# Row-halved score matmuls, a split ninth product, a longer lead and a new order of turns in a fused RWKV and attention kernel

## The chip, the cores and the metric

The kernel runs on one core of one Trainium2 chip. The metric is the device time of one execution in microseconds (us). Shorter is better. TensorE is called PE, VectorE DVE, ScalarE ACT, GpSimd POOL, and SyncE, which issues nearly all DMAs, SP.

## What is computed

Two branches are computed from one layer-normed input of 2 x 1024 tokens by 128 channels, and both are added to the input. The first branch is RWKV: a WKV recurrence over time, gates, and a channel mix. The second branch is attention with 16 heads of 8 channels and weights mixed from experts. Cut to what matters here:

```python
q, k, v = (shp(q), shp(k), shp(v))       # (2, 16, 1024, 8) each
attn = jax.nn.softmax(jnp.einsum('bhsd,bhtd->bhst', q, k), axis=-1)
ctx = jnp.einsum('bhst,bhtd->bhsd', attn, v)
x = x + rwkv(xn, ...) + svd_moe(ctx, ...)
```

## The kernel before, in words

Two heads make a pair, and there are 16 pairs. Every value of q and k is split into three bf16 parts (main, rest, rest of the rest). A float32 product of 8 channels is so made from 9 products of parts, in 72 rows of contraction. The parts are written to DRAM (`store_parts`, L421) and loaded back per pair, replicated, into `q_op` and `k_op` (`load_pair`, L382): 96 rows are used for the first scores and 99 for the second ones. There are four buffer sets for the pairs (`SETS`).

Scores are computed twice.

- **A scores** (`fill_place`, L1078, the matmul on L1091) have queries on the partitions. One bf16 matmul gives 128 queries x 512 keys in one of three PSUM banks (5, 6, 7). DVE reduces it to its maximum (`read_place`, L973, the reduction on L986). A pair has 32 of these and one more turn (k = 2), in which PE transposes the maxima of the pair before (L1084), and DVE copies them out (L982). POOL splits them into three bf16 parts (`split_max`, L557), and SP places them as rows 96 to 98 of `q_op` (`place_max`, L393), against rows of ones in `k_op`.
- **B scores** (`scores`, L1161, the matmul on L1166) have keys on the partitions and already hold the subtraction of the maximum. Two matmuls fill two banks, and ACT takes the exponential of both in one instruction (`exps`, L801). A second two banks make the double buffer.
- **Values** (`values`, L1170, the matmul on L1176): float32 matmuls of 32 columns, in four column groups of the array for 2 heads x 2 halves of the queries. They accumulate in bank 4, which ACT copies at the end of a pair (`copy_ctx`, L807). SP stores it (`store_ctx`, L407), and it is loaded again at the end (`load_contexts`, L459).

The main loop has 128 steps, 8 for each pair, in iterations of four pairs, which are 32 steps. The order is written out by hand. `one_step` (L1180) issues for PE in each step: A turn 0, B scores of head 0, A turn 1, B scores of head 1, A turn 2, the values of the step before, A turn 3 (in one step of eight also a fifth turn), then possibly a product.

```python
fill_turn(it, todo[0])
if step == 0:
    pe.wait_ge(max_in[j % 2], (it * 2 + j // 2 + 1) * 16 * PARTS)
scores(p, j, step, 0)
fill_turn(it, todo[1])
scores(p, j, step, 1)
fill_turn(it, todo[2])
```

Products (`product`, L1138) are the float32 matmuls of the RWKV branch. An iteration has seven steps with one product (mean, var, cr and ck0 to ck3, at steps 17, 18, 22, 23, 25, 26 and 27) and one step (29) with cv, which is four in a row. They take a turn in the same rotation of three banks. The RWKV branch also gives DVE two scans after the A turns of each of the steps 2, 6 and 12 (L945), and work to ACT and POOL in many steps (`branch`).

Each A turn waits until DVE, or whoever takes a product, has read the turn three places earlier (`wait_for_bank`, L344). PE takes its instructions in order, so everything behind such a wait stands too. The A scores run ahead of the B scores by one pair and `LEAD` = 12 turns. This lead of 45 turns is computed before the loop, beside the projections of the RWKV branch (L1112, L1100).

SP has one queue in program order. Before the loop it stores the parts of batch 0, loads pairs 0 to 2 (12 DMAs), stores the parts of batch 1 (8 DMAs), stages v of pair 0 (`stage_v`, L400) and places the maxima of pair 0. In the loop it has 13 DMAs for each pair.

Of the kernel before, what the change touches and what calls it, by code (L numbers as in the profile page):

```python
# [6 lines left out]
P = 128  # L7
TILES = B * T // P
CHUNK = 512
# [6 lines left out]
ROWS = PARTS * PARTS * HD  # L16
MAX_ROW = 96
# [3 lines left out]
LEAD = 12  # L21
SPLIT_STEP = 5
# [24 lines left out]
def build(nc, x, cols, mats, rows, gw1, gb1, gw2, gb2, out):  # L47
# [4 lines left out]
    with ctx:  # L52
# [55 lines left out]
        q_op = sb("q_op", [P, SETS, 2, T], BF16)  # L108
        k_op = sb("k_op", [P, SETS, 2, T], BF16)
# [14 lines left out]
        ctx_dram = nc.dram_tensor("ctx_dram", [PAIRS, 4, HD + 1, CHUNK], F32).ap()  # L124
# [131 lines left out]
        op_in = [[sem(f"op_in{s}{e}") for e in range(2)] for s in range(SETS)]  # L256
# [67 lines left out]
        for t in range(SETS * KEY_TILES):  # L324
            at = A_PLACES + LEAD
            here = places(at + A_PLACES * t // KEY_TILES, at + A_PLACES * (t + 1) // KEY_TILES)
            place_turns.append(range(len(turns), len(turns) + len(here)))
            turns += here
            turns += [name for name, step in PRODUCT_STEP.items() if step == t]
        assert (len(turns) + 1) % 3 == 0  # L330
# [50 lines left out]
        def _(sp):  # L381
            def load_pair(p, s):  # L382


                for e in range(2):
                    sp.dma_start(q_op[0:ROWS, s, e, :],
                                 bass.AP(q_dram.tensor, (p * 2 + e) * (PARTS * HD * T),
                                         [[0, PARTS], [T, PARTS * HD], [1, T]])).then_inc(op_in[s][e], 16)
                    sp.dma_start(k_op[0:ROWS, s, e, :],
                                 bass.AP(k_dram.tensor, (p * 2 + e) * (SLOTS * HD * T),  # L390
                                         [[HD * T, PARTS], [T, PARTS * HD], [1, T]])).then_inc(op_in[s][e], 16)

            def place_max(p, s):  # L393

                sp.wait_ge(max_parts_ready, p + 1)
                for i in range(PARTS):
                    sp.dma_start(q_op[MAX_ROW + i:MAX_ROW + i + 1, s, :, :],
                                 max_parts[:, s % 2, i, :]).then_inc(max_in[s % 2], 16)

            def stage_v(p, s):  # L400

                for e in range(2):
                    sp.dma_start(v_op[:, s % 2, :, e, 0:HD],
                                 V[:, bass.ds(p, 1), :, HD * e:HD * e + HD].rearrange("p o k d -> p (o k) d")
                                 ).then_inc(v_in[s % 2], 16)

            def store_ctx(p, s):  # L407
                sp.wait_ge(ctx_copied, p + 2)
                for g in range(4):
                    sp.dma_start(bass.AP(ctx_dram.tensor, (p * 4 + g) * ((HD + 1) * CHUNK),  # L410
                                         [[CHUNK, HD + 1], [1, CHUNK]]),
                                 ctx_sb[32 * g:32 * g + HD + 1, s % 2, :]).then_inc(ctx_out[s % 2], 16)
# [8 lines left out]
            def store_parts(b, t):  # L421

                for slot in range(SLOTS if t else PARTS):
                    sp.dma_start((k_dram if t else q_dram)[b * HEADS:(b + 1) * HEADS, slot, :, :],
                                 parts[:, t, slot % PARTS, 2 * b:2 * b + 2, :].rearrange("p n t -> p (n t)")
# [24 lines left out]
            def rest(p, j, it):  # L450
                if not isinstance(p, int) or p + 3 < PAIRS:
                    sp.wait_ge(b_ready, p * 16 + 1)
                    load_pair(p + 3, (j + 3) % SETS)
                if not isinstance(p, int) or p + 1 < PAIRS:
                    sp.wait_ge(pv_done, p * 8 + 1)
                    stage_v(p + 1, (j + 1) % SETS)
                    place_max(p + 1, (j + 1) % SETS)

            def load_contexts(b):  # L459

                for s in range(2):
                    sp.wait_ge(ctx_out[s], 64 * (PAIRS // 4) * (b + 1) + 1)
                for hs in range(2):
                    at = (b * (HEADS // 2) * 4 + hs) * (HD + 1) * CHUNK
                    head_step = 2 * (HD + 1) * CHUNK
# [23 lines left out]
        def _(pool):  # L489
# [21 lines left out]
            g.memset(q_op[:, :, :, :], 0.0).then_inc(cleared, 1)  # L511
# [759 lines left out]
```

## Time and profile before

| what | us |
|---|---|
| median of 3 runs (527.71 to 529.12) | 528.16 |
| span of the profiled execution, first to last instruction | 526.2 |
| median less span | 1.96 |
| PE busy, of the span | 470.9 (89%) |
| DVE busy | 407.4 (77%) |
| ACT busy | 356.4 (68%) |
| POOL busy | 183.4 (35%) |

The profiled execution has no other time on record than its span. Busy time counts the time in which at least one instruction of an engine was under way. Matmuls overlap one another, so their mean duration is longer than the time from the start of one to the start of the next. A line of the timeline merges instructions of one kind that follow each other, with their count behind an x.

### The profile page before, as it was taken

What the parts mean: (1) busy time and instruction counts of PE and PEld (TensorE: products, weight loads), DVE (VectorE), ACT (ScalarE), POOL (GpSimd) and SP (SyncE); (2) the same over time, 40 slices, a digit from 0 to 9 for tenths busy, and PEclk for the clock granted to TensorE, in tenths of its full rate; (3) what the DMA queues carried; (4) which work ended last, traced back from release to release, by engine and by line L of the source; (5) the groups of instructions that cost most, each with busy time, mean ns of one, the idle gap of its engine ahead of it and who ended that gap; (6) DMA issues with size and microseconds to landing.
All of it is one profiled execution on the core that took longest, in us unless ns stands there. A gap on an engine that the chain in (4) does not pass through costs nothing.

```text
span 526.2 us, 8110 instructions
## 1 busy us (share of the span) xinstructions
PE 470.9 (89%) x2358; PEld 160.8 (31%) x2358; DVE 407.4 (77%) x668; ACT 356.4 (68%) x452; POOL 183.4 (35%) x214
## 2 busy tenths in 40 slices
PE   5339379999999999999999999999999999999992
PEld 3115123232233332222333322223333223232252
DVE  3578989999888868998887689998876899981022
ACT  3865212578968756789788567887775678878851
POOL 9556900331534221315432303153323031634200
PEclk9859769999999999999999999999999999999996
DMA  6001326110111110101101001111010111010205
GB/s 211 0 1 56 121 75 208 30 25 12 48 32 27 33 25 10 46 24 33 36 20 38 19 15 41 27 30 43 14 45 11 22 37 12 1 13 1 87 7 159
DMA packets 49289, 22.25 MB, mean 42 GB/s; under 512 B 36532, under 2 KB 40756, under 8 KB 49268
## 3 DMA queue, kind: packets, MB, share of 16 engines
q1 hardware_dynamic: 48736, 21.83, 15.3%
q10 hardware_dynamic: 532, 0.16, 0.3%
q8 instruction: 11, 0.18, 0.2%
q14 instruction: 10, 0.08, 0.0%
HBM read 14.31 MB, written 6.42 MB: 39 GB/s over the span
## 4 chain that ended last, share of the span: by engine, by line
PE 69%; DVE 16%; ACT 5%; issue 5%; DMA 3%; POOL 1%; SPq 1%; DVEq 0%; POOLq 0%; ACTq 0%
PE banks L1091 19%; PE banks L1176 19%; PE banks L1166 17%; DVE neg_half L986 6%; PE banks L1159 3%; ACT probs L804 3%; PE banks L1155 3%; DVE run L945 2%; DVE probs L917 1%; PE banks L1112 1%; PE banks L1100 1%; DMA x_sb<-in_x_dram 1%; DVE parts L921 1%; DVE parts L919 1%; DVE parts L915 1%
## 5 line engine op out<-in xcount | busy, mean ns | idle before, releaser
L986 DVE TENSOR_REDUCE neg_half<-banks 128x1 f32<-128x512 f32 x512 | 323.7, 685 | 46.1 <-PE banks L1091 44.3
L804 ACT ACTIVATE probs<-banks 128x1024 f32<-128x1024 f32 x256 | 247.5, 1021 | 74.4 <-PE banks L1166 73.6
L1091 PE MATMUL banks<-k_op,q_op 96*128 96x512 bf16 x512 | 181.2, 384 | 19.7 <-DVE V L937 11.4
L1166 PE MATMUL banks<-q_op,k_op 99*128 99x512 bf16 x512 | 151.5, 379 | 1.2 <-DMA q_op<-max_parts 0.6
L1176 PE MATMUL banks<-probs,v_op 128*32 128x512 f32 x1024 | 136.4, 605 | 0.4 <-ACT probs L804 0.4
L1091 PEld LDWEIGHTS banks<-k_op,q_op 96*128 96x128 bf16 x512 | 43.6, 97 | 170.0 <-DVE neg_half L986 126.3
L1166 PEld LDWEIGHTS banks<-q_op,k_op 99*128 99x128 bf16 x512 | 49.0, 98 | 65.3 <-issue 11.9
L1176 PEld LDWEIGHTS banks<-probs,v_op 128*32 128x32 f32 x1024 | 20.1, 108 | 53.5 <-issue 52.3
L643 POOL TENSOR_TENSOR qk_f<-qk_f 128x512 f32<-128x512 f32 x12 | 12.5, 1039 | 52.6 <-ACT qk_f L789 52.6
L968 DVE TENSOR_TENSOR rec<-banks,parts 128x512 f32<-128x512 f32 x4 | 2.8, 692 | 34.6 <-PE banks L1155 34.6
L564 POOL TENSOR_TENSOR max_parts<-max_rows,zero_rows 16x128 bf16<-16x128 f32 x16 | 7.1, 444 | 56.7 <-DVE max_rows L982 56.3
L597 POOL TENSOR_TENSOR xc<-run 128x512 f32<-128x512 f32 x4 | 4.2, 1039 | 48.4 <-DVE run L945 48.4
L742 ACT ACTIVATE sq<-banks 128x512 f32<-128x512 f32 x4 | 2.4, 598 | 22.0 <-PE banks L1100 22.0
L1159 PE MATMUL banks<-xc,mat_sb 128*128 128x512 f32 x32 | 16.8, 606 | 0.0
L602 POOL TENSOR_TENSOR qk_f<-qk_f 128x512 f32<-128x512 f32 x4 | 5.1, 1276 | 33.4 <-ACT qk_f L757 33.4
L789 ACT ACTIVATE qk_f<-banks 128x512 f32<-128x512 f32 x12 | 7.2, 597 | 11.2 <-PE banks L1159 11.2
L1112 PE MATMUL banks<-hT,u_s 128*128 128x512 f32 x24 | 13.2, 631 | 0.0
L1100 PE MATMUL banks<-hT,u_s 128*128 128x512 f32 x24 | 12.6, 607 | 0.0
L610 POOL TENSOR_TENSOR hT<-qk_f,hT 128x512 f32<-128x512 f32 x4 | 5.1, 1278 | 19.4 <-ACT hT L763 19.4
L606 POOL TENSOR_TENSOR hT<-qk_f,parts 128x512 f32<-128x512 f32 x4 | 5.1, 1280 | 18.9 <-ACT qk_f L763 18.9
L1015 DVE TENSOR_TENSOR parts<-parts 128x512 f32<-128x512 f32 x4 | 2.8, 693 | 11.4 <-ACT parts L830 11.4
L579 POOL TENSOR_TENSOR xc<-xc,run 128x512 f32<-128x512 f32 x8 | 9.3, 1183 | 5.6 <-ACT xc L784 5.6
(163 smaller groups left out, 456.0 us busy)
## 6 DMA issues: line engine op xcount, KB each, us to landing
q_op<-q_dram SPq DMA_DIRECT2D x32, 144.0 KB
k_op<-k_dram SPq DMA_DIRECT2D x32, 144.0 KB
k_dram<-parts SPq DMA_DIRECT2D x10, 256.0 KB, 3.9
parts<-ctx_dram SPq DMA_DIRECT2D x8, 256.0 KB, 4.2
mat_sb<-in_mats_dram SPq DMA_DIRECT2D x2, 768.0 KB, 7.7
q_dram<-parts SPq DMA_DIRECT2D x6, 256.0 KB, 3.2
ctx_dram<-ctx_sb SPq DMA_DIRECT2D x64, 18.0 KB
x_sb<-in_x_dram SPq DMA_DIRECT2D x4, 256.0 KB, 5.6
```

The source lines that it names most:

```text
L579: g.tensor_tensor(mix_in[i][:, :, :], mix_in[i][:, :, :], prev, ALU.add).then_inc(mixed, 1)
L643: g.tensor_tensor(kk[i][:, :, :], kk[i][:, :, :], kk[i][:, :, :], ALU.mult).then_inc(kk_ready, 1)
L804: a.activation(probs[:, (2 * step + e) % 4, :, :], banks[:, 2 * e:2 * e + 2, :], ACT.Exp).then_inc(b_read, 1)
L945: v.tensor_tensor_scan(out_[:, b, 1:], c0[:, b, :], data1, out_[:, b, 0:1], op0, op1).then_inc(done, 1)
L986: v.tensor_reduce(neg_half[:, s, u:u + 1], src, axis=AX.X, op=ALU.max, negate=True).then_inc(a_read, 1)
L1091: mm(dst, q_op[0:MAX_ROW, s, e, P * c:P * c + P], k_op[0:MAX_ROW, s, e, CHUNK * h:CHUNK * h + CHUNK], start=True, stop=True).then_inc(a_re ...
L1100: mm(project_bank(m), w_mix[:, i, 1, :], hT[:, n // 2, at:at + CHUNK], start=False, stop=True).then_inc(kvr_ps, 1)
L1112: mm(project_bank(m), w_mix[:, i, 0, :], hT[:, n // 2, at:at + CHUNK], start=True, stop=False)
L1155: last = mm(dst, mat(f"cv{i}"), flat(kk[i]), start=(i == 0), stop=(i == 3))
L1159: mm(dst, mat(name), flat(mix_in[1]), start=True, stop=True).then_inc(ck_ps, 1)
L1166: last = mm(bank(2 * e + h), k_op[0:MAX_ROW + PARTS, s, e, P * step:P * step + P], q_op[0:MAX_ROW + PARTS, s, e, CHUNK * h:CHUNK * h + CHU ...
L1176: last = mm(banks[g:g + 32, PV_BANK, :], v_op[:, s % 2, step, e, :], probs[:, (2 * step + e) % 4, h, :], start=(step == 0), stop=(step == ...
```

## The change

A matmul of the A scores has 64 rows instead of 96: 8 of the 9 products of parts, with head 0 in rows 0 to 63 and head 1 in rows 64 to 127. The two heads of one block of queries and keys are neighbouring turns. The ninth product (8 rows) and the three rows of the maximum stand in `q_tail` and `k_tail`, 35 rows in each half. The B scores are four matmuls where they were two: for both heads the 64 rows of the main part, then for both the 35 rows of the tail, accumulated in the same banks. One call of `scores` now makes both heads for one half of the queries, and ACT reads as much as before in each instruction. The A scores leave out the smallest product, so the maximum is that of an approximated score; what is subtracted cancels in the softmax.

In a step, PE issues B scores of half 0, turns 0 and 1 (and in one step of eight the turn k = 2), B scores of half 1, turns 2 and 3, values, product. The lead is one pair and 17 turns. `load_pair` issues 12 DMAs instead of 4 for a pair, `place_max` 6 instead of 3, `stage_v` 1 instead of 2, and `store_ctx` 1 instead of 4. The loads of head 1 in the loop stand behind `place_max`. POOL splits the maxima after its step 4, not 5.

```diff
-LEAD = 12
-SPLIT_STEP = 5
+LEAD = 17
+UNITS = 16
+LEAD_UNITS = 8
+SPLIT_STEP = 4
...
+        def unit_places(unit):
+            return (2 * unit, 2 * unit + 1) if unit == 0 else (2 * unit + 1, 2 * unit + 2)
+
+        def place_of(k):
+            u = k if k < 2 else k - 1
+            return u % 2, u // 4, u // 2 % 2
...
-            at = A_PLACES + LEAD
-            here = places(at + A_PLACES * t // KEY_TILES, at + A_PLACES * (t + 1) // KEY_TILES)
+            for half in range(2):
+                ahead, unit = divmod(LEAD_UNITS + 2 * (t % KEY_TILES) + half, UNITS)
+                pair = t // KEY_TILES + 1 + ahead
+                here.append([(pair, k) for k in unit_places(unit)])
+                if unit == 0:
+                    here[-1].append((pair, 2))
...
-            def load_pair(p, s):
-                for e in range(2):
-                    sp.dma_start(q_op[0:ROWS, s, e, :],
+            def load_pair(p, s, heads=(0, 1)):
+                for e in heads:
+                    sp.dma_start(q_main[here, s, :], bass.AP(q_dram.tensor, q_at, [[0, 2], [T, PARTS * HD], [1, T]])
+                                 ).then_inc(main_in[s][e], 16)
+                    sp.dma_start(k_main[here, s, :], bass.AP(k_dram.tensor, k_at, [[HD * T, 2], [T, PARTS * HD], [1, T]])
+                                 ).then_inc(main_in[s][e], 16)
+                    sp.dma_start(q_main[then, s, :], bass.AP(q_dram.tensor, q_at, [[T, 2 * HD], [1, T]])
+                                 ).then_inc(main_in[s][e], 16)
+                    sp.dma_start(k_main[then, s, :], bass.AP(k_dram.tensor, k_at + 2 * HD * T, [[T, 2 * HD], [1, T]])
+                                 ).then_inc(main_in[s][e], 16)
+                    sp.dma_start(q_tail[last, s, :], bass.AP(q_dram.tensor, q_at + 2 * HD * T, [[T, HD], [1, T]])
+                                 ).then_inc(tail_in[s], 16)
+                    sp.dma_start(k_tail[last, s, :], bass.AP(k_dram.tensor, k_at + 4 * HD * T, [[T, HD], [1, T]])
+                                 ).then_inc(tail_in[s], 16)
...
-                if u % 16 == 0:
-                    pe.wait_ge(op_in[s][e], (it + pair // SETS + 1) * 32)
-                mm(dst, q_op[0:MAX_ROW, s, e, P * c:P * c + P],
-                   k_op[0:MAX_ROW, s, e, CHUNK * h:CHUNK * h + CHUNK],
+                if k < 2:
+                    pe.wait_ge(main_in[s][e], (it + pair // SETS + 1) * 64)
+                mm(dst, q_main[HALF * e:HALF * (e + 1), s, P * c:P * c + P],
+                   k_main[HALF * e:HALF * (e + 1), s, CHUNK * h:CHUNK * h + CHUNK],
...
-                for h in range(2):
-                    last = mm(bank(2 * e + h), k_op[0:MAX_ROW + PARTS, s, e, P * step:P * step + P],
-                              q_op[0:MAX_ROW + PARTS, s, e, CHUNK * h:CHUNK * h + CHUNK], start=True, stop=True)
+                for q_rows, k_rows, used in ((q_main, k_main, HALF), (q_tail, k_tail, MAX_ROW + PARTS)):
+                    for e in range(2):
+                        last = mm(bank(2 * h + e), k_rows[HALF * e:HALF * e + used, s, P * step:P * step + P],
+                                  q_rows[HALF * e:HALF * e + used, s, CHUNK * h:CHUNK * h + CHUNK],
+                                  start=(q_rows is q_main), stop=(q_rows is q_tail))
...
-                fill_turn(it, todo[0])
                 if step == 0:
-                    pe.wait_ge(max_in[j % 2], (it * 2 + j // 2 + 1) * 16 * PARTS)
+                    pe.wait_ge(tail_in[j], (it + 1) * 64)
+                    pe.wait_ge(max_in[j % 2], (it * 2 + j // 2 + 1) * 32 * PARTS)
                 scores(p, j, step, 0)
-                fill_turn(it, todo[1])
+                for turn in todo[0]:
+                    fill_turn(it, turn)
                 scores(p, j, step, 1)
-                fill_turn(it, todo[2])
+                for turn in todo[1]:
+                    fill_turn(it, turn)
...
-                for turn in todo[3:]:
-                    fill_turn(it, turn)
```

## Rows read from the trace of the kernel before

**Rows 1.** The page: its span, and the chain that ended last, by engine.
```profile
span 526.2 us, 8110 instructions
...
PE 69%; DVE 16%; ACT 5%; issue 5%; DMA 3%; POOL 1%; SPq 1%; DVEq 0%; POOLq 0%; ACTq 0%
```

**Rows 2.** Windows, one iteration: stretch, length, busy us of PE, PEld, DVE, ACT, POOL, clock, DMA.
```profile
191.60:295.90 104.30, 102.02 (x539) 31.79 (x539) 88.20 (x146) 78.09 (x93) 33.75 (x42) 1.00 0.12 28
```

**Rows 3.** The page's groups: busy us, mean ns of one, idle before it and releaser.
```profile
L986 DVE TENSOR_REDUCE neg_half<-banks 128x1 f32<-128x512 f32 x512 | 323.7, 685 | 46.1 <-PE banks L1091 44.3
...
L1176 PE MATMUL banks<-probs,v_op 128*32 128x512 f32 x1024 | 136.4, 605 | 0.4 <-ACT probs L804 0.4
```

**Rows 4.** Timeline of a plain step, PE and DVE: start us, length us, engine, line.
```profile
206.19 1.06 PE L1176 MATMUL banks<-probs,v_op 128*32 128x512 f32 x8
207.19 0.60 PE L1091 MATMUL banks<-k_op,q_op 96*128 96x512 bf16 x2
...
207.61 2.48 DVE L986 TENSOR_REDUCE neg_half<-banks 128x1 f32<-128x512 f32 x4 [0.35 <-PE banks L1091]
207.63 0.60 PE L1166 MATMUL banks<-q_op,k_op 99*128 99x512 bf16 x2
...
208.72 0.38 PE L1091 MATMUL banks<-k_op,q_op 96*128 96x512 bf16 x1
...
209.03 1.07 PE L1176 MATMUL banks<-probs,v_op 128*32 128x512 f32 x8
```

**Rows 5.** Timeline, a turn that waited for its bank, and the reads before it.
```profile
249.86 5.63 DVE L986 TENSOR_REDUCE neg_half<-banks 128x1 f32<-128x512 f32 x9 [0.35 <-PE banks L1091]
...
250.61 0.39 PE L1091 MATMUL banks<-k_op,q_op 96*128 96x512 bf16 x1
```

**Rows 6.** Timeline of PE, a step with one product.
```profile
288.06 1.07 PE L1176 MATMUL banks<-probs,v_op 128*32 128x512 f32 x8
...
289.29 1.02 PE L1159 MATMUL banks<-xc,mat_sb 128*128 128x512 f32 x2
290.15 0.38 PE L1091 MATMUL banks<-k_op,q_op 96*128 96x512 bf16 x1
```

**Rows 7.** Timeline of DVE: the copy of the transposed maxima, and the two scans of step 6.
```profile
219.45 0.28 DVE L982 COPY max_rows<-banks 16x128 f32<-16x128 f32 x1
...
222.90 1.39 DVE L945 TENSOR_TENSOR_SCAN run<-qk_f,run 128x256 f32<-128x256 f32 x2
```

**Rows 8.** Timeline of PE: values of steps 1 and 30, 30 again, and 20 of the last iteration.
```profile
101.21 1.07 PE L1176 MATMUL banks<-probs,v_op 128*32 128x512 f32 x8
...
196.48 1.06 PE L1176 MATMUL banks<-probs,v_op 128*32 128x512 f32 x8
...
300.76 0.64 PE L1176 MATMUL banks<-probs,v_op 128*32 128x512 f32 x4
...
473.20 1.06 PE L1176 MATMUL banks<-probs,v_op 128*32 128x512 f32 x8
```

**Rows 9.** Timeline of the SP queue before the loop: start us, length of the issues us.
```profile
60.50 0.94 SPq L386 DMA_DIRECT2D q_op<-q_dram  x1
...
62.30 0.70 SPq L386 DMA_DIRECT2D q_op<-q_dram  x1
63.05 0.71 SPq L389 DMA_DIRECT2D k_op<-k_dram  x1
...
76.79 3.19 SPq L424 DMA_DIRECT2D q_dram<-parts  x3
...
83.93 5.27 SPq L403 DMA_DIRECT2D v_op<-V  x2
...
94.56 1.88 SPq L397 DMA_DIRECT2D q_op<-max_parts  x3
```

**Rows 10.** Timeline of PE: the first B scores of the kernel.
```profile
97.83 0.59 PE L1166 MATMUL banks<-q_op,k_op 99*128 99x512 bf16 x2
```

**Rows 11.** Waits of the SP queue: us in total, times, longest us.
```profile
SPq L397 <- POOL max_parts L570: 138.5, 16, 13.7
```

More of the change, by code:

```diff
@@ L106, in build @@
         V = sb("V", [P, PAIRS, KEY_TILES, 2 * HD])
-        q_op = sb("q_op", [P, SETS, 2, T], BF16)
-        k_op = sb("k_op", [P, SETS, 2, T], BF16)
+        q_main = sb("q_main", [P, SETS, T], BF16)
+        k_main = sb("k_main", [P, SETS, T], BF16)
+        q_tail = sb("q_tail", [P, SETS, T], BF16)
+        k_tail = sb("k_tail", [P, SETS, T], BF16)
         v_op = sb("v_op", [P, 2, KEY_TILES, 2, 32])
@@ L255, in build @@
         parts_out = [sem(f"parts_out{b}") for b in range(B)]
-        op_in = [[sem(f"op_in{s}{e}") for e in range(2)] for s in range(SETS)]
+        main_in = [[sem(f"main_in{s}{e}") for e in range(2)] for s in range(SETS)]
+        tail_in = [sem(f"tail_in{s}") for s in range(SETS)]
         v_in = [sem(f"v_in{s}") for s in range(2)]
@@ L452, in rest @@
                     sp.wait_ge(b_ready, p * 16 + 1)
[L453 removed]
+                    load_pair(p + 3, (j + 3) % SETS, heads=(0,))
                 if not isinstance(p, int) or p + 1 < PAIRS:
@@ L510, in _ @@
                 g.memset(ctx_sb[:, s, 0:1], 0.0).then_inc(ctx_out[s], 1)
-            g.memset(q_op[:, :, :, :], 0.0).then_inc(cleared, 1)
+            g.memset(q_tail[:, :, :], 0.0).then_inc(cleared, 1)
             pool.wait_ge(cleared, 1)
             pool.wait_ge(keys_cleared, 1)
-            g.memset(k_op[MAX_ROW:MAX_ROW + PARTS, :, :, :], 1.0).then_inc(ones_set, 1)
+            for e in range(2):
+                ones = g.memset(k_tail[HALF * e + MAX_ROW:HALF * e + MAX_ROW + PARTS, :, :], 1.0)
+            ones.then_inc(ones_set, 1)
             pool.wait_ge(ones_set, 1)
@@ L801, in exps @@
             def exps(p, step):
-                for e in range(2):
-                    act.wait_ge(b_ready, p * 16 + 2 * step + e + 1)
-                    a.activation(probs[:, (2 * step + e) % 4, :, :], banks[:, 2 * e:2 * e + 2, :],
+                for h in range(2):
+                    act.wait_ge(b_ready, p * 16 + 2 * step + h + 1)
+                    a.activation(probs[:, (2 * step + h) % 4, :, :], banks[:, 2 * h:2 * h + 2, :],
                                  ACT.Exp).then_inc(b_read, 1)
@@ L996, in one_step @@
             def one_step(t, it):
-                for turn in place_turns[t]:
+                for turn in (*place_turns[t][0], *place_turns[t][1]):
                     read_place(it, *turns[turn], turn_bank(turn))
```

71 lines of the change are left out of this document (37 added, 34 removed).

## The prediction

> **What bounds the kernel now.** I read the page first. The chain that ended last lies 69% on PE and 16% on DVE [rows 1]. The windows of one whole iteration of the loop sharpen this: of 104.3 us PE is busy 102.0, DVE 88.2 and ACT 78.1, at a granted clock of 1.00, which is 2.4 GHz [rows 2]. So the loop is PE's. The groups then show what DVE does: 512 maxima of 685 ns each, and nearly all of its idle time before them (44.3 of 46.1 us) ended with an A score of PE [rows 3].
>
> The timeline of a plain step gives the gaps from which all that follows is made [rows 4]. I write V for the start of the values.
>
> - From V to the next bf16 matmul: 207.19 - 206.19 = 1.00.
> - From one bf16 matmul to the next: (207.63 - 207.19) / 2 = 0.22.
> - From a bf16 matmul to V: 209.03 - 208.72 = 0.31.
> - The step: 209.03 - 206.19 = 2.84. It is 1.00 + 7 x 0.22 + 0.31 = 2.85, so PE never stands.
> - From an A matmul to the start of its maximum: 207.61 - 207.19 = 0.42, and 0.43 with rounding. Maxima in a queue start 0.62 apart, (5.63 - 0.685) / 8 [rows 5].
> - From the end of a maximum to the matmul that waited for its bank: the maximum of 249.86 ends at 250.545, the matmul starts at 250.61 [rows 5], 0.07.
>
> **The change, part by part.**
>
> *Two heads side by side.* No row shows two matmuls in different row halves. Bounds for such a pair: 0.22 if they run together, 0.43 if one follows the other [rows 4]. The nearest rows are the values: 1024 matmuls of 605 ns have PE busy for 136.4 us [rows 3], and eight of them end after 1.07 us [rows 4], so tiles of the array in different columns do run together. I take 0.22. The B scores are then two pairs for each half, 0.43, as long as the two matmuls they replace. Two A scores take the time of one. PE's own sum for a step becomes 1.00 into B, 0.43, 0.22 for turns 0 and 1, 0.43, and 0.31 from turns 2 and 3 to V: 2.39. DVE's is 4 x 0.62 = 2.48. On throughput alone a step would fall from 2.84 to DVE's 2.48.
>
> *The new order.* It makes a chain that the old order did not have. Turn 3 needs the bank of turn 0 of the same step. Before, turn 0 stood 0.22 or less after turn 3 of the step before; now values and B scores of half 0 stand between. From V = 0: B of half 0 at 1.00, turns 0 and 1 at 1.43, maximum of turn 0 at 1.86 to 2.55, turn 1 read from 2.48. B of half 1 at 1.65, turn 2 at 2.08 (its bank, turn 3's of the step before, was free at 1.56). Turn 3 waits for turn 0's bank until 2.61. Behind it in PE's queue stand the values, at 2.61 + 0.31 = 2.92. The next step starts only there, so a plain step takes **2.92**, not 2.48: turn 3 stands 0.53 after turn 2, and DVE, whose last maximum ends about 1.45 after V, stands 0.4 until turn 0 is there. The gain of PE is lost in a wait, and 0.08 more.
>
> Terms of this chain that no row shows are the changes between tile shapes. Before, 0.09 (0.31 - 0.22) is lost into the values and 0.14 (1.00 - 0.86) out of them, with 0.86 the two float32 passes of a product [rows 6]. With row halves each can be nothing or twice this: 2.69 to 3.15 for a step. I keep the rows as they are.
> The Trainium skill, "TensorEngine Tiling (Array Packing)", section Tiling Modes, says that changing the tiling mode drains the engine. By that rule nothing of 0.09 and 0.14 goes, and a product between values and 64-row scores pays once more; the trace shows the former and no row the latter.
>
> *Steps with a product.* The product moves between values and B, into the chain: 0.86 [rows 6] as before. Product to B is now a change of shape: 0 to 0.14, I take 0.10. Seven times 0.96 = 6.7 an iteration. For cv, 4 x 0.86 = 3.44; DVE then reads it and adds to it, 1.4, before it can read turn 0, as before: in all 4.1.
>
> *Scans.* Two scans take 1.39 [rows 7]. They stand before the maximum of turn 0, which DVE could start at 1.86; it starts at 2.81, 0.95 late, twice an iteration. In step 12 the turn k = 2 has already shifted DVE and it is 0.52: 2.4 in all.
>
> *The turn k = 2.* It takes a bank between turns 1 and 2. Turn 2 then waits for turn 0 (2.61) and turn 3 for turn 1, 2.48 + 0.685 + 0.07 = 3.23; V at 3.54, 0.62 more, four times an iteration: 2.5. DVE's copy of 0.28 [rows 7] is inside this.
>
> *An iteration* is 32 x 2.92 + 6.7 + 4.1 + 2.4 + 2.5 = 109.1, against 300.76 - 196.48 = 104.3 [rows 8].
>
> *Before the loop.* SP issues 36 loads instead of 12. One takes 0.75 from issue to issue where nothing presses [rows 9]; 12 took 16.3 because the bytes pressed, and the bytes stay. They start at 60.50 and end at 87.6 instead of 76.8. Behind them stand the 8 stores, 7.1, and v, one issue of about 2.6: 97.3. Then the maxima, six issues of 0.63, to 101.1, instead of 96.4. The first B scores came 1.4 after that [rows 9, 10]: 102.5. Other side: PE has five more A turns, 5 x 0.62 = 3.1, and head 1 of pair 0 lands about 1 us later, which the paired A matmuls partly win back; the last turn of the lead is issued near 102.4. Both meet at 102.6. From there the banks are full and I follow the reads: V of step 1 at 107.7 instead of 101.2 [rows 8], **+6.5** (3.5 to 10, as the stores press less or the DMA of v takes all of its 5.3).
>
> *The loop proper*, from V of step 1 to V of step 20 of the last iteration, took 473.2 - 101.2 = 372.0 [rows 8]. Now it is 3 x 109.1 and 19 steps: 19 x 2.92 + 2.4 (scans) + 2 x 0.62 + 2 x 0.96 = 61.1. In all 388.4, **+16.4**.
>
> *The end.* One step more has no A scores, -0.5; six changes of shape, +0.6; one store instead of four before the last contexts, between -1 and +0.5. I take -0.4.
>
> *Costed at nothing.* In the loop SP has 20 issues for a pair instead of 13, some 19 us of 24. It stood 138.5 us before the maxima [rows 11]; that idle time covers it. The maxima are ready three and a half steps before their use, the loads of head 1 a third of a pair. If the cover were gone, one pair would wait for the seven added issues, 5 us, sixteen times. Smaller memsets lie beside the input's DMAs. ACT keeps its instructions; its heaviest steps (9 to 12) lag about 0.35 each, and 0.9 of lag are free.
>
> **Sum.** 526.2 + 6.5 + 16.4 - 0.4 = 548.7 for the span. The median of the runs lies 1.96 above the span of the profile: 550.7, say **551**, 4.3% slower.
>
> **Rivals.**
>
> *The wait does not bind, and DVE's pace decides: faster.* One place: turn 0 behind the values. If the result of turn 0 came before DVE's store of read-out work ended, a plain step would be 2.48: 0.44 x 115 = 51 less than mine, 500. If DVE never stood at all, an iteration would take its 88.2 busy us [rows 2], 3.6 iterations of 21 us less than mine: 475. The terms besides the plain step cost 6.5 - 0.4 + (16.4 - 115 x 0.08) = 13.3, so it is faster from a step of 2.84 - 13.3 / 115 = 2.72 downwards. For it: two changes of shape that cost nothing give 2.69. Against it: every term of the chain has its row, and with three banks DVE has at most 3 x 0.62 = 1.87 of work in store, while from turn 3 to the next turn 0 PE needs 1.74 and the result another 0.43.
> This is the reading of the Trainium skill, "TensorEngine Tiling (Array Packing)", section Performance Considerations, under PSUM Bottleneck: with tiling, emptying PSUM may become the bound. The trace of before has PE as the bound and can't show it.
>
> *The halves do not run together* (the change does not do what it says). Then B takes 0.86 for each half and a step is 3.68. That is 0.84 x 115 = 97 more than before in the plain part, about 6 less since the scans hide, 9 more in the last 11 steps, 7 before the loop: some 634. Against it are the values; for it only that no row has row halves.
>
> **Chances.** Forecast 0.77, with 524 to 579 as its ends: chain 2.69 to 3.15 (-26 to +26), and a little for the start. Halves in turn 0.08, more than 579 for other reasons 0.03, the wait not binding 0.12. The range 524 to 579 leaves out two in ten. About 0.3% is what a measurement of this kernel can tell from no change, 526.6 to 529.7: faster 0.13 with the low end of my own case, same 0.03, slower 0.84.
>
> **What would show it.** In the timeline of a plain step: V to V 2.9; turns 0 and 1 at one time, each pair of B scores too; turn 3 some 0.5 after turn 2, PE's wait put down to DVE's maximum; DVE standing 0.4 before turn 0, put down to PE. Windows of an iteration: 109 us, PE busy below 95, DVE 88 still. First B scores near 102.5, values of step 1 near 107.7. It is wrong if plain steps are under 2.75 or over 3.15, if the two heads' matmuls start 0.2 apart, or if PE waits in the loop for q_tail, q_main or v_op.

## The result, and the profile after

The changed kernel takes 553.06 us (median of 4 runs, 551.5 to 555.46), the kernel before on the same chip 528.25. The ratio is 1.0477 (95% interval 1.0438 to 1.0516): **slower by 4.8%**. The forecast was 551. The profiled execution has a span of 551.6 us, against 526.2.

The chain that ended last, by engine, stands against [rows 1]:

```profile
span 551.6 us, 9333 instructions
...
PE 60%; DVE 25%; issue 5%; DMA 4%; ACT 3%; SPq 2%; DVEq 0%; ACTq 0%
```

PE's share of it fell from 69% to 60% and DVE's rose from 16% to 25%. The groups say between which lines (against [rows 3]):

```profile
L1020 DVE TENSOR_REDUCE neg_half<-banks 128x1 f32<-128x512 f32 x512 | 318.7, 681 | 69.1 <-PE banks L1124 68.2
...
L1124 PE MATMUL banks<-k_main,q_main 64*128 64x512 bf16 x512 | 146.3, 386 | 41.4 <-DVE neg_half L1020 17.0
...
L1200 PE MATMUL banks<-q_main,k_main 64*128 64x512 bf16 x512 | 100.3, 385 | 1.0 <-ACT probs L837 0.8
```

DVE stands 68.2 us for the A scores of PE, where it stood 44.3, and the A scores (L1124) now stand for the maxima of DVE. Each engine waits for the other, and neither is full. The window of one iteration, from the values (V) of step 30 to the same point 32 steps on (columns as in [rows 2]), says the same of the whole loop:

```profile
210.58:320.14 109.56, 102.06 (x667) 27.52 (x666) 86.53 (x146) 77.90 (x93) 34.77 (x43) 1.00 0.14 34
```

The iteration takes 109.56 us instead of 104.3, at the same clock. DVE has 1.7 us less to do. PE's busy time of 102.06 only looks unchanged: a matmul of 0.38 us counts as busy to its end, though the next could start after 0.22, so of a wait of about half a us only 0.13 shows as idle time. The prediction had named a busy time below 95 as a sign; that sign failed, while its signs for the plain step all held. How much room there is, the timeline of a plain step shows (start us, length us, engine, line; the rows of before are [rows 4]):

```profile
219.35 1.07 PE L1211 MATMUL banks<-probs,v_op 128*32 128x512 f32 x8
220.35 0.39 PE L1200 MATMUL banks<-q_main,k_main 64*128 64x512 bf16 x2
220.57 0.38 PE L1200 MATMUL banks<-q_tail,k_tail 35*128 35x512 bf16 x2
220.79 0.38 PE L1124 MATMUL banks<-k_main,q_main 64*128 64x512 bf16 x2
...
221.01 0.38 PE L1200 MATMUL banks<-q_main,k_main 64*128 64x512 bf16 x2
221.23 0.38 PE L1200 MATMUL banks<-q_tail,k_tail 35*128 35x512 bf16 x2
...
221.44 0.90 PE L1124 MATMUL banks<-k_main,q_main 64*128 64x512 bf16 x2
...
222.27 1.06 PE L1211 MATMUL banks<-probs,v_op 128*32 128x512 f32 x8
```

and DVE beside it:

```profile
221.21 2.48 DVE L1020 TENSOR_REDUCE neg_half<-banks 128x1 f32<-128x512 f32 x4 [0.44 <-PE banks L1124]
```

- V to V is 222.27 - 219.35 = 2.92.
- Two matmuls in different row halves end together: a line of two has a length of 0.38 or 0.39, and the next line starts 0.22 later.
- Turns 2 and 3 are the line at 221.44. It lasts 0.90, not 0.38, because turn 3 starts 0.52 after turn 2. It waits for the bank of turn 0.
- DVE's four maxima take 2.48. Then it stands 0.44, for PE. The 2.48 holds the whole of the last maximum (0.685), so they start (2.48 - 0.685) / 3 = 0.60 apart. The prediction had 0.62, a mean over nine maxima of which one had waited for its A score. DVE alone would need 4 x 0.60 = 2.40 for a step, not 2.48.

**Where the 25.4 us of span are** (551.6 - 526.2), against [rows 8]: V of step 1 starts at 109.48 instead of 101.21, +8.3. From there to V of step 20 of the last iteration (498.78) it is 389.3 instead of 372.0, +17.3. The rest is 52.8 instead of 53.0, -0.2.

### The profile page after: what moved, and what is told of

Its sections match the earlier page's. It is cut to its first block, busy times and chain, and to the rows that moved or that the text cites. A ratio compares the mean times of both kernels' runs of the same rounds, so it can differ in the third digit from the quotient of the medians.

```text
span 551.6 us, 9333 instructions
## 1 busy us (share of the span) xinstructions
PE 476.5 (86%) x2870; PEld 143.7 (26%) x2870; DVE 400.1 (73%) x668; ACT 356.4 (65%) x452; POOL 184.7 (33%) x215
## 3 DMA queue, kind: packets, MB, share of 16 engines
q1 hardware_dynamic: 51104, 24.85, 16.4%
## 4 chain that ended last, share of the span: by engine, by line
PE 60%; DVE 25%; issue 5%; DMA 4%; ACT 3%; SPq 2%; DVEq 0%; ACTq 0%
PE banks L1211 20%; DVE neg_half L1020 17%; PE banks L1124 14%; PE banks L1200 12%; PE banks L1192 3%; PE banks L1188 3%; DVE run L978 2%; ACT probs L837 2%; PE banks L1145 2%; PE banks L1133 1%; DMA x_sb<-in_x_dram 1%; DMA k_main<-k_dram 1%; PE banks L1073 1%; PE banks L1181 1%; PE banks L1178 1%
## 5 line engine op out<-in xcount | busy, mean ns | idle before, releaser
L1020 DVE TENSOR_REDUCE neg_half<-banks 128x1 f32<-128x512 f32 x512 | 318.7, 681 | 69.1 <-PE banks L1124 68.2
L1124 PE MATMUL banks<-k_main,q_main 64*128 64x512 bf16 x512 | 146.3, 386 | 41.4 <-DVE neg_half L1020 17.0
L1200 PE MATMUL banks<-q_main,k_main 64*128 64x512 bf16 x512 | 100.3, 385 | 1.0 <-ACT probs L837 0.8
L1200 PE MATMUL banks<-q_tail,k_tail 35*128 35x512 bf16 x512 | 99.4, 381 | 0.0
L1124 PEld LDWEIGHTS banks<-k_main,q_main 64*128 64x128 bf16 x512 | 36.5, 95 | 147.8 <-DVE neg_half L1020 107.8
L1200 PEld LDWEIGHTS banks<-q_main,k_main 64*128 64x128 bf16 x512 | 24.9, 94 | 121.6 <-ACT probs L837 77.7
L1200 PEld LDWEIGHTS banks<-q_tail,k_tail 35*128 35x128 bf16 x512 | 25.7, 95 | 13.2 <-issue 0.2
L843 ACT COPY ctx_sb<-banks 128x512 f32<-128x512 f32 x16 | 9.4, 586 | 8.6 <-PE banks L1211 8.6
L1145 PE MATMUL banks<-hT,u_s 128*128 128x512 f32 x24 | 14.0, 669 | 0.0
L1133 PE MATMUL banks<-hT,u_s 128*128 128x512 f32 x24 | 13.0, 623 | 0.0
L601 POOL TENSOR_TENSOR max_parts<-max_res,zero_rows 16x128 bf16<-16x128 f32 x16 | 11.6, 727 | 1.3
```

Of the source, the lines that this page charges most:

```text
L601: g.tensor_tensor(m1, res_, zero_rows[:, :], ALU.add).then_inc(max_part, 1)
L1020: v.tensor_reduce(neg_half[:, s, u:u + 1], src, axis=AX.X, op=ALU.max, negate=True).then_inc(a_read, 1)
L1124: mm(dst, q_main[HALF * e:HALF * (e + 1), s, P * c:P * c + P], k_main[HALF * e:HALF * (e + 1), s, CHUNK * h:CHUNK * h + CHUNK], start=True ...
L1133: mm(project_bank(m), w_mix[:, i, 1, :], hT[:, n // 2, at:at + CHUNK], start=False, stop=True).then_inc(kvr_ps, 1)
L1145: mm(project_bank(m), w_mix[:, i, 0, :], hT[:, n // 2, at:at + CHUNK], start=True, stop=False)
L1200: last = mm(bank(2 * h + e), k_rows[HALF * e:HALF * e + used, s, P * step:P * step + P], q_rows[HALF * e:HALF * e + used, s, CHUNK * h:CHU ...
```

## The experiments

"Plain step" below is V to V of a step that has neither a product, scans nor the turn k = 2. Every ratio is against the kernel before on the same chip. The first three tell apart what the new order does from what the row halves do.

**e1: all four turns of a step in one block behind the values, then the B scores.** The turns stay in the order in which they rotate through the banks.

```diff
+                for turn in todo[0]:
+                    fill_turn(it, turn)
                 (waits of step 0)
                 scores(p, j, step, 0)
-                for turn in todo[0]:
-                    fill_turn(it, turn)
                 scores(p, j, step, 1)
                 for turn in todo[1]:
                     fill_turn(it, turn)
```

> The changed kernel, with one order undone: PE issues turns 0 and 1 before the B scores of half 0, and both B scores stand together before turns 2 and 3. Theory (turn 3 waits for turn 0's bank, and values and B scores stand between them): turn 0 comes 0.43 earlier after the values, turn 3 at 2.18 instead of 2.61, and a plain step is 2.49, which is also DVE's pace (4 x 0.62). Steps with a product, PE's own, about 3.5 (2.39 + 1.06); an iteration about 100 instead of 109.6; the time about 519 (505 to 530), faster than both kernels. Rival (the time lies in the row halves themselves, in their changes of shape or in lost concurrency): the plain step stays at 2.92 or within 0.1 of it, the time at 550.

Measured: 523.77 us (5 runs), ratio 0.9914 (0.9882 to 0.9945). The timeline of PE in a plain step:

```profile
213.94 1.06 PE L1211 MATMUL banks<-probs,v_op 128*32 128x512 f32 x8
214.94 0.39 PE L1124 MATMUL banks<-k_main,q_main 64*128 64x512 bf16 x2
215.16 0.38 PE L1200 MATMUL banks<-q_main,k_main 64*128 64x512 bf16 x2
...
216.04 0.46 PE L1124 MATMUL banks<-k_main,q_main 64*128 64x512 bf16 x2
...
216.43 1.07 PE L1211 MATMUL banks<-probs,v_op 128*32 128x512 f32 x8
```

V to V is 2.49, and the iteration takes 99.7 us instead of 109.56. One call of the B scores was taken out from between turn 3 and the next turn 0, and 0.43 us a step came back. DVE has no gap left, but it is not its pace that sets the 2.49, which would be 2.40. Turn 3 starts at 216.04 + 0.46 - 0.39 = 216.11, which is 1.17 after turn 0, and 0.32 ahead of the next V; from V to the next turn 0 it is 1.00. The bank's wait is still in the step, only nothing is added to it. The total missed the expectation by 4 to 5 us: those lie ahead of the loop (e5).

**e2: the order of before with the row halves.** Turn 0, B of half 0, turn 1, B of half 1, turn 2, values, turn 3.

```diff
-                todo = place_turns[t]
+                todo = [*place_turns[t][0], *place_turns[t][1]]
+                fill_turn(it, todo[0])
                 scores(p, j, step, 0)
+                fill_turn(it, todo[1])
                 scores(p, j, step, 1)
+                fill_turn(it, todo[2])
                 (values)
+                for turn in todo[3:]:
+                    fill_turn(it, turn)
```

> The changed kernel with the turns in the slots that they had before: turn 0, B scores, turn 1, B scores, turn 2, values, turn 3. Theory: turn 3 and the next turn 0 follow the values at once, nothing waits for a bank, and PE's sum decides: 1.00 + 0.22 (turns 3 and 0 together) + 0.43 + 0.22 + 0.43 + 0.31 = 2.61 for a plain step; an iteration about 98.5, the time about 515 (505 to 530). Rival (row halves cost the time whatever the order): plain step 2.9, the time near 550.

Measured: 523.23 us (6 runs), ratio 0.9922 (0.9895 to 0.9949), an iteration of 100.99 us. A plain step of PE:

```profile
224.48 1.07 PE L1211 MATMUL banks<-probs,v_op 128*32 128x512 f32 x8
225.48 0.39 PE L1124 MATMUL banks<-k_main,q_main 64*128 64x512 bf16 x2
...
226.14 0.38 PE L1124 MATMUL banks<-k_main,q_main 64*128 64x512 bf16 x1
226.15 0.59 PE L1200 MATMUL banks<-q_main,k_main 64*128 64x512 bf16 x2
...
226.97 1.06 PE L1211 MATMUL banks<-probs,v_op 128*32 128x512 f32 x8
```

The step is 2.49, not the 2.61 that I expected. I had given turn 1 a slot of its own, but it and the B scores that follow lie in different halves and start at 226.14 and 226.15. The **row halves do bring something in this order**: 2.49 against 2.84. They bring no more because turn 2 (226.65) waits for the bank of turn 3 (225.48), 1.17 us, and V follows 0.32 later: the same 2.49 as in e1. The total is 8 above the expected 515; an iteration took 100.99 instead of 98.5, and V of step 1 came at 111.16.

**e3: the kernel before with the new order and no row halves.**

```diff
-                fill_turn(it, todo[0])
                 scores(p, j, step, 0)
-                fill_turn(it, todo[1])
+                for turn in todo[:2]:
+                    fill_turn(it, turn)
                 scores(p, j, step, 1)
-                fill_turn(it, todo[2])
+                for turn in todo[2:]:
+                    fill_turn(it, turn)
                 (values, then nothing)
```

> The kernel before (96 and 99 rows, no halves, its lead of 12 and its DMAs), with only the new order in a step: B scores, turns 0 and 1, B scores, turns 2 and 3, values. Theory: the same chain as in the changed kernel, since it holds only one B score call and the values: from values 1.00, B scores 0.43, turn 0 to its bank free 1.18, 0.31 to the values: 2.92 for a plain step, though PE has no slack won. An iteration about 107 to 109, the time about 540 to 548, slower than before by some 3%. Rival (the slowdown comes from the halves): plain step 2.84 and the time 528.

Measured: 548.25 us (4 runs), ratio 1.0388 (1.0353 to 1.0422), an iteration of 110.0 us. A plain step of PE:

```profile
238.91 1.07 PE L1176 MATMUL banks<-probs,v_op 128*32 128x512 f32 x8
239.90 0.60 PE L1166 MATMUL banks<-q_op,k_op 99*128 99x512 bf16 x2
240.35 0.60 PE L1091 MATMUL banks<-k_op,q_op 96*128 96x512 bf16 x2
240.78 0.59 PE L1166 MATMUL banks<-q_op,k_op 99*128 99x512 bf16 x2
...
241.83 1.07 PE L1176 MATMUL banks<-probs,v_op 128*32 128x512 f32 x8
```

The step is 2.92, as in the changed kernel; the iteration and the total lie just above what was expected. Edit for edit: the order alone costs 548.25 - 527.9 = 20 us of the 25. Everything but the order (e2: halves, lead and DMAs) brings some 4 to 5. Together they are worse than the order alone: an iteration is 0.4 shorter, but V of step 1 comes at 109.48 instead of 103.30. The halves bring next to nothing in the new order because PE's time is not what the chain waits for. They shorten what PE does inside the wait for turn 0's bank.

**e4: e1 with the turn k = 2 late.** Behind the values only turns 0 and 1, the rest after both calls of B.

```diff
+                for turn in todo[0][:2]:
+                    fill_turn(it, turn)
                 scores(p, j, step, 0)
                 scores(p, j, step, 1)
-                for turn in todo[1]:
+                for turn in (*todo[0][2:], *todo[1]):
                     fill_turn(it, turn)
```

> As e1_turns_first, and the turn k = 2 (transpose of the maxima) is issued behind both B scores. In e1 it waits for DVE's small reduction with the B scores behind it. Theory: the four steps of an iteration with this turn shrink from about 3.1 to about 2.9 and nothing else moves: 1 us less an iteration, 3 us in all below e1. Rival (the B scores behind the transpose were not needed earlier): the same time as e1 within 0.5 us.

Measured: 523.03 us (5 runs), ratio 0.992 (0.9892 to 0.9947), an iteration of 99.80 us against e1's 99.74. My expectation failed and the rival held. A k = 2 step took 3.23 (e1: 3.22). Some steps won (the one with a product and k = 2 takes 4.14 instead of 4.28), others lost: the step after the scans of step 12 takes 3.98 instead of 3.72. Part of that is in the scans themselves, 0.95 and 0.85 instead of 0.82 and 0.84, beside work of POOL (see e7).

e1 and e4 win 4.5 us an iteration on the kernel before (104.3), and yet only some 4 to 5 us in all. What is lost lies ahead of the loop: V of step 1 comes at 112.56 in e1 and 109.11 in e4 instead of 101.21. Windows of that stretch in the changed kernel, as in [rows 2]:

```profile
104.00:110.00 6.00, 6.00 (x28) 2.16 (x31) 5.56 (x10) 3.91 (x4) 0.00 (x0) 0.50 0.15 38
```

The granted clock is 0.50, which is 1.2 GHz, in the first B steps. In the kernel before it is 1.00 in the same stretch. What PE did before it fell: the last seven turns of the longer lead have no projections of the RWKV branch beside them, so PE had one A score per maximum of DVE and little else.

**e5: e4 with the projections spread further over the lead.**

```diff
-PROJECT_EARLY, PROJECT_FROM, PROJECT_GAP = 4, 2, 5
+PROJECT_EARLY, PROJECT_FROM, PROJECT_GAP = 4, 2, 6
```

> e4_turns_first_k_late, with the projections before the loop spread over six A turns each instead of five, so that they reach to the end of the longer lead. Theory: in the changed kernel the last seven turns of the lead have no projection beside them, PE then has one bf16 matmul in 0.6 us, the granted clock falls to 1.2 GHz, and the first two steps of the loop run at half speed. With the projections spread the clock stays at 1.00 over the first steps, the values of step 1 come about 2 us earlier and the time falls from 523 to 521. Rival (the clock falls for another reason, or DVE is the bound there anyway): the clock is 0.5 in the first steps again, or the time stays within 0.5 of e4.

Measured: 519.91 us (4 runs), ratio 0.985 (0.9801 to 0.9898). The window of e4,

```profile
104.00:108.00 4.00, 3.64 (x18) 1.59 (x16) 2.97 (x6) 2.01 (x3) 0.00 (x0) 0.50 0.06 12
```

and of e5:

```profile
104.00:108.00 4.00, 3.01 (x22) 1.49 (x23) 3.81 (x7) 2.55 (x4) 2.43 (x5) 1.00 0.03 3
```

At 1.00 PE does 22 matmuls in the stretch in which it did 18. From the first A score to V of step 2 it is 43.9 us instead of 46.4; the 2.5 us are most of the 3.1 by which the medians differ. PE has the same instructions in both kernels. The two were measured on different chips, and the intervals of their ratios touch; it is the traces that show the difference.

**e6: e5 with head 1 of pair 0 loaded by ACT's queue.** In the changed kernel the second A score waits for data: `72.91 [2.31 <-DMA k_main<-k_dram]`, 2.31 us. I thought that SP's queue issued the loads of head 1 too late.

```diff
+            act.wait_ge(parts_out[0], PARTS_OUT)
+            for there, dram, at, step in ((q_main, q_dram, PARTS * HD * T, 0), (k_main, k_dram, SLOTS * HD * T, HD * T)):
+                act.dma_start(there[HALF:HALF + 2 * PARTS * HD, 0, :],
+                              bass.AP(dram.tensor, at, [[step, 2], [T, PARTS * HD], [1, T]])).then_inc(main_in[0][1], 16)
+                act.dma_start(there[HALF + 2 * PARTS * HD:2 * HALF, 0, :],
+                              bass.AP(dram.tensor, at + 2 * step, [[T, 2 * HD], [1, T]])).then_inc(main_in[0][1], 16)
```

SP leaves these four out.

> e5_projections_spread, and the four main loads of head 1 of pair 0 are issued by ACT's queue beside SP's loads of head 0. Theory: the second A score of the kernel waits 2.3 to 2.7 us for these loads, because they stand seventh to tenth in SP's queue; issued in parallel they land before the first A score needs them, all A scores of the lead start 2 to 2.5 us earlier, and the time falls from 521 to about 519. Rival (the loads are held up by the transfer itself, not by the issue): the wait stays near 2.3 us and so does the time.

Measured: 519.92 us (4 runs), ratio 0.9832 (0.9792 to 0.9872), no gain on e5. The A scores that waited, in e5

```profile
70.52 0.61 PE L1124 MATMUL banks<-k_main,q_main 64*128 64x512 bf16 x2 [2.88 <-DMA k_main<-k_dram]
```

and in e6:

```profile
73.86 1.01 PE L1131 MATMUL banks<-k_main,q_main 64*128 64x512 bf16 x3 [14.50 <-DMA k_main<-k_dram]
```

In e6 the first A score itself waits, until 11.8 us after the first load was issued (62.03); in e5 the first one runs 8.3 us after it (58.78) and the second 11.7. So the rival held: what both heads need is there no sooner, whichever queue issues the loads. Issuing them from a second queue made head 0 later and head 1 no earlier as far as the A scores show.

**e7: e5 with a lead of 15 turns instead of 17.**

```diff
-LEAD = 17
+LEAD = 15
-LEAD_UNITS = 8
+LEAD_UNITS = 7
```

> e5_projections_spread with a lead of 15 instead of 17 turns. Theory: two maxima less before the loop, 2 x 0.62 = 1.2 us, and half a step more with A scores near the end, up to 0.5 us: the time 0.7 to 1.2 us below e5. The turn k = 2 moves behind turn 3 of its step; if PE then waits for q_tail at the first step of a pair, it is slower by up to 1 us in each pair instead (535).

Measured: **517.45 us** (4 runs), ratio 0.9798 (0.9759 to 0.9837), 2.5 us less than e5 where 0.7 to 1.2 was expected, though the intervals of the two overlap. It is the best version of this study, 2.0% faster than the kernel before. Its iteration:

```profile
199.82:299.24 99.42, 94.59 (x669) 27.77 (x668) 86.75 (x146) 77.68 (x94) 34.66 (x43) 1.00 0.15 38
```

Counted from the first A score, the trace is 2.6 us shorter than e5's: 1.0 up to V of step 1 (two turns less of lead, as expected), 0.9 from there to V of step 20 of the last iteration, 0.6 behind it. An iteration wins 0.4, nearly all of it in the step after the scans of step 12 (3.63 instead of 3.98). The scans and POOL's splitting of the maxima still meet there, but the other way round: in e5 the two scans take 0.95 and 0.85 and POOL loses little (0.69 instead of 0.42 for one operation), in e7 they take 0.73 and 0.71 and the first operation of POOL takes 1.38 instead of 0.45.

**e8: the changed kernel with its values one place earlier.** This was to test the chain itself. Turns 0 and 1, B of half 1, values, turns 2 and 3, B of half 0.

```diff
-                for turn in todo[0]:
+                for turn in todo[0][:2]:
                     fill_turn(it, turn)
                 scores(p, j, step, 1)
-                for turn in todo[1]:
-                    fill_turn(it, turn)
                 (values)
+                for turn in (*todo[0][2:], *todo[1]):
+                    fill_turn(it, turn)
```

> The changed kernel, B scores first as it has them, but the values of the step before are issued ahead of turns 2 and 3 instead of behind them (and the turn k = 2 between values and turn 2). Theory: what costs the time is that values AND the B scores stand between turn 3 and the next turn 0; here only B scores stand there, turn 3 finds its bank free, and a plain step is DVE's 2.49, as in e1. A step with a product is about 3.4. The time 512 to 522. Rival (what e1 won came from moving the first B scores behind turns 0 and 1, so that they are wanted later): here nothing of that is moved, a plain step stays at 2.92 and the time at 550.

Measured: 559.21 us (4 runs), ratio 1.0618 (1.0591 to 1.0645). The expectation fell twice. First, a plain step of PE stayed at 2.92:

```profile
220.21 1.07 PE L1211 MATMUL banks<-probs,v_op 128*32 128x512 f32 x8
221.21 0.39 PE L1124 MATMUL banks<-k_main,q_main 64*128 64x512 bf16 x2
...
221.87 0.90 PE L1124 MATMUL banks<-k_main,q_main 64*128 64x512 bf16 x2
222.47 0.52 PE L1200 MATMUL banks<-q_main,k_main 64*128 64x512 bf16 x2
...
223.13 1.06 PE L1211 MATMUL banks<-probs,v_op 128*32 128x512 f32 x8
```

The wait had only moved. Turn 1 now needs the bank of turn 2, which runs at 221.21, right behind the values. Turn 1 has its bank 1.18 later (0.43 to the maximum, 0.685 for it, 0.07 to the matmul), at 222.39. Behind it stand the B scores of half 1 (0.43) and the gap of 0.31 into the values: 223.13. The **revised theory**: for every turn, the third next can start 1.18 after it, and everything that PE must do in order outside that stretch is added. In all these orders the values with their gaps lie outside it, 1.31 (1.00 + 0.31), and each call of the B scores that lies outside adds 0.43. With none outside it gives 1.18 + 1.31 = 2.49 (e1, e2), with one 2.92 (the changed kernel, e3, e8). I had looked at one turn of the four only.

Second, once an iteration the scans of step 12 met POOL. The timeline there:

```profile
256.89 4.15 DVE L978 TENSOR_TENSOR_SCAN run<-qk_f,run,hT 128x256 f32<-128x256 f32 x2
...
258.02 1.25 POOL L643 TENSOR_TENSOR hT<-qk_f,hT 128x512 f32<-128x512 f32 x1
...
259.24 1.25 POOL L644 TENSOR_TENSOR hT<-hT,parts 128x512 f32<-128x512 f32 x1
```

Two scans took 4.15 us (0.94 and 3.29) where they take 1.39 [rows 7]. PE stood 3.12 for them, and behind this its granted clock fell for a while:

```profile
263.00:268.00 5.00, 5.00 (x29) 1.06 (x29) 3.15 (x6) 3.03 (x4) 2.31 (x2) 0.66 0.17 51
```

Steps 14 and 15 take 6.77 and 4.01, and steps 12 to 15 together 16.8, against 12.6 in the changed kernel. Product steps are cheaper in e8 (3.57 against 3.98, and the one with cv 6.14 against 7.32), which makes up for it in a whole iteration (109.28). The last iteration pays for the scans and ends before the products have paid it back: V of its step 20 comes 3.8 us later than in the changed kernel. The profiled spans differ by 4.1, the medians by 6.2; the rest is open.

**e9: e8 with the projections spread as in e5** (PROJECT_GAP 6).

> e8_values_before_turn2 with the projections before the loop spread over six turns each, as in e5. Theory: the clock stays at 1.00 in the first steps, 2 to 3 us less than e8. Rival: no difference, if DVE is the bound there in this order.

Measured: 557.29 us (5 runs), ratio 1.0583 (1.0557 to 1.061), 1.9 us less than e8 (2 to 3 expected), with a granted clock of 1.00 from 104 to 112 where e8 has 0.78 and 0.80. The gain of e5 stands in another order too.

**e10: both calls of B ahead of turn 0.** The revised theory gives a number of its own here: two calls outside the stretch, 2.49 + 2 x 0.43.

```diff
                 scores(p, j, step, 0)
+                scores(p, j, step, 1)
                 for turn in todo[0]:
                     fill_turn(it, turn)
-                scores(p, j, step, 1)
                 for turn in todo[1]:
                     fill_turn(it, turn)
```

> The changed kernel with both B scores ahead of turns 0 and 1: B, B, turns 0 and 1, turns 2 and 3, values. The theory in its second form, after e8: for every turn, the third next one waits 1.18 after its start (0.43 matmul, 0.685 maximum, 0.07), and PE must also do, in order, whatever stands outside that stretch; a step is 1.18 + 1.31 (values with the gaps around them) + 0.43 for each call of B scores that stands outside. Here both do: 1.18 + 1.31 + 0.87 = 3.36 for a plain step, an iteration near 123, the time near 600. Rival (the changed kernel's 2.92 has another cause, with PE's work the same in both): plain step 2.92 and 551.

Measured: 601.23 us (2 runs), ratio 1.1411 (1.1336 to 1.1486), an iteration of 121.9 us. A plain step of PE:

```profile
232.66 1.07 PE L1211 MATMUL banks<-probs,v_op 128*32 128x512 f32 x8
233.65 0.39 PE L1200 MATMUL banks<-q_main,k_main 64*128 64x512 bf16 x2
...
234.54 0.59 PE L1124 MATMUL banks<-k_main,q_main 64*128 64x512 bf16 x3
235.70 0.39 PE L1124 MATMUL banks<-k_main,q_main 64*128 64x512 bf16 x1 [0.57 <-DVE neg_half L1020]
236.01 1.06 PE L1211 MATMUL banks<-probs,v_op 128*32 128x512 f32 x8
```

236.01 - 232.66 = 3.35, against 3.36 worked out. Turn 3 starts 235.70 - 234.54 = 1.16 after turn 0. Only turn 2 lies in between, so PE's idle time now shows openly, 0.57 before turn 3, put down to DVE's maximum. In the changed kernel most of the same wait was hidden from this view by matmuls that overlap it. With steps of 2.49, 2.92 and 3.36 and an iteration of 99.7, 109.56 and 121.9, place and price of the chain are shown.

## Why the prediction was right, step by step

| step of the prediction | forecast | measured |
|---|---|---|
| pair of matmuls in two row halves | 0.22 | 0.22 |
| maxima in a queue, start to start | 0.62 | 0.60 |
| plain step | 2.92 | 2.92 |
| step with a product, more than plain | 0.96 | 1.06 |
| cv, more than plain | 4.1 | 4.40 |
| two scans, step 12 | 0.95, 0.52 | 0.76, 0.34 |
| turn k = 2 | 0.62 | 0.60 |
| iteration | 109.1 | 109.56 |
| before V of step 1 | +6.5 | +8.3 |
| loop proper | +16.4 | +17.3 |
| end | -0.4 | -0.2 |

- **The new order.** Right in mechanism, place and size, for both halves of the argument: the order makes the chain (e3, 2.92 without halves), and with nothing added to the bank's wait a step is 2.49 (e1 and e2). That this is also the 2.48 that the prediction gave to DVE is a coincidence: DVE's own pace is 2.40, and no order tried here reached it. What the prediction did not see is how general the chain is. It named "turn 3 needs the bank of turn 0", and this reading led to the wrong expectation for e8.
- **Changes of shape.** Keeping the rows of 0.09 and 0.14 was right: V to B is 220.35 - 219.35 = 1.00 and the end of a step 0.31. The rule of the Trainium skill ("TensorEngine Tiling (Array Packing)", section Tiling Modes, a change of mode drains the engine) fits: nothing of the 1.00 and 0.31 went, and the product paid once more.
- **Product steps.** The term was too small by 0.10. The product in the changed kernel:

```profile
270.16 1.13 PE L1178 MATMUL banks<-qk_f,mean_w 128*128 128x512 f32 x2
271.21 0.39 PE L1200 MATMUL banks<-q_main,k_main 64*128 64x512 bf16 x2
```

  From product to B it is 1.05. In e3, which has no row halves, it is 0.96, and before, where the product stood behind an A turn instead of behind the values, 0.86 [rows 6]. So the product pays 0.10 on its way in, which I had costed at nothing, and 0.09 on its way out, for which I took 0.10. The first is not a matter of the values alone: in e8 the product stands behind 64-row A turns, and from product to B it is 1.06 all the same. Both look like changes of shape, before and behind the product.
- **Scans.** Mis-sized by 0.2 each. My timetable put whole durations one behind the other, but neighbours in DVE's queue overlap by 0.08 to 0.09: a maximum lasts 0.685 and the next starts after 0.60. After V at 222.27 the scans start 1.34 later instead of 1.42, and the next maximum 2.64 later instead of 2.81.
- **The 7 product steps, cv, scans and k = 2** add up: 32 x 2.92 + 7 x 1.06 + 4.40 + 1.86 + 2.4 = 109.5.
- **Before the loop, the step that failed.** I made SP's queue the bound: 36 issues of 0.75 to 87.6, the maxima placed by 101.1. The queue in the changed kernel:

```profile
61.56 0.82 SPq L410 DMA_DIRECT2D q_main<-q_dram  x1
...
82.50 0.29 SPq L420 DMA_DIRECT2D k_tail<-k_dram  x1
...
88.58 0.81 SPq L434 DMA_DIRECT2D v_op<-V  x1
...
98.61 4.12 SPq L428 DMA_DIRECT2D q_tail<-max_parts  x6
```

  A load of fewer rows has a shorter issue, 0.28 to 0.67 for most, so the 36 are out by 82.8, and after v's issue at 88.58 the queue issues nothing until the maxima are ready, at 98.61. The path that ended last is the one that I had called "the other side", the A turns: the second score waits 2.31 for head 1 of pair 0, the maxima are copied at 95.87 instead of 92.17, and the last turn of the lead starts at 103.31, right ahead of the first B scores at 103.91. That my two paths met at 102.6 hid the error, so the size of this term is partly luck. Where the 8.3 lie: the first load itself started 1.1 later (61.56 instead of 60.50), from there to the first B scores it took 5.0 more (42.35 instead of 37.33; my sum had 4.8), and from those to V of step 1 2.2 more (5.57 instead of 3.38; my sum had 1.7). The start of the first load lies anywhere from 58.4 to 62.5 in the traces of this study, also where the program ahead of it is the same (61.78 in e3), so the first part can't be put down to the change. In the last part the granted clock is 0.50, which the prediction had not looked for. e9 against e8 shows what such a clock is worth there, 3.55 instead of 4.42; how much of the changed kernel's 2.2 it makes is not shown.
- **Costed at nothing.** SP's added issues in the loop: PE never waited for q_tail, q_main or v_op there, as said.
- **The rivals.** "DVE's pace decides" is out for this order. In e1, e2 and e4 DVE has no gap in a plain step, but the step of 2.49 is still set by the bank, 0.09 above DVE's 2.40. The bound that the Trainium skill names ("TensorEngine Tiling (Array Packing)", section Performance Considerations, PSUM Bottleneck) is nearly met there. "The halves do not run together" is out: lines of two end after 0.38 and 0.39.

## What to carry to other kernels

Where an engine works in order through a short rotation of buffers, write down for every place of the rotation when the buffer is free again (here 1.18 later) and what the engine must do outside that stretch; the sum is the step as long as it is longer than what each engine needs on its own, and faster instructions inside the stretch bring nothing. Look at all places of the rotation before moving one, since the wait moves along. A longer lead that leaves PE with little to do costs twice, by its own turns and by the clock at which the next stage starts.

## What the runs showed of the hardware that I had not expected

- **The clock.** In the stretch from 104 to 108 of e4 and e5 the granted clock is 0.50 and 1.00 (1.2 and 2.4 GHz) with the same instructions in the kernel. Only the place of the projections differs. It came to 2.5 us of 520. The same fall shows in e8 from 263 to 268 (0.66), right after PE had stood for 3.12.
- **DVE's scans and POOL exclude one another.** In step 12 of the changed kernel POOL's small operation takes 1.56 us while the scans run; its median is 0.44. The timeline of DVE and POOL:

```profile
145.58 1.37 DVE L978 TENSOR_TENSOR_SCAN run<-qk_f,run,hT 128x256 f32<-128x256 f32 x2
...
145.64 1.56 POOL L601 TENSOR_TENSOR max_parts<-max_res,zero_rows 16x128 bf16<-16x128 f32 x1
```

  In e8 it is the other way round: POOL is there first (256.84, against 256.89), and the two scans take 0.94 and 3.29 us instead of 0.73 each. The Trainium skill, "SBUF — State Buffer", section SBUF: two separate sides, states it as a lock: a DVE instruction with two SBUF inputs and a GpSimd instruction that reads SBUF exclude each other, and the first one holds the ports to its end. The rows agree in both directions. The second scan of e8 starts at 257.76 and ends only behind two operations of POOL that start after it (258.02 and 259.24). Why POOL went first twice is open.
- **Matmuls of different rows overlap even when they are of different kinds.** In e2 an A turn in one half and the B scores in the other start at 226.14 and 226.15.
- **Loads of few rows are cheap to issue** (0.28 to 0.67 us for most of them), but what the first two A scores need is there only 11.7 us after the first issue from one queue (e5) and 11.8 from two (e6).
